# Halving the masked softmax of layer three and reordering the engine queues of a four-layer graph network

## What is computed

```python
x = layernorm(x + L0(x, adj)); x = layernorm(x + L1(x, adj))
x = layernorm(x + L2(x, adj)); x = layernorm(x + L3(x, adj))
# L0, L1: graph attention with one head (softmax over 256 neighbours, masked by adj)
# L2 ("layer three", index 2 in the names): 4 heads of 32 features
def L2(x, adj):
    q, k, v = (x @ Wq + bq), (x @ Wk + bk), (x @ Wv + bv)      # split in 4 heads
    scores = einsum('bnhd,bmhd->bhnm', q, k) / sqrt(32)
    attn = softmax(where(adj | eye, scores, min))              # 4 x 256 x 256 per graph
    return relu(einsum('bhnm,bmhd->bnhd', attn, v) @ Wo + bo)
# L3: gated relational convolution; adj here holds 0 and 1 only
```

## Time and profile before

| | |
|---|---|
| median of 3 runs | 487.91 us (486.52 to 494.0) |
| the profiled execution's own time | 486.33 us |
| its span, first to last instruction | 484.5 us |
| mean granted TensorE clock | 0.995 of full speed |
| DMA | 38.79 MB, mean 80 GB/s |

### The profile page before, as it was taken

One profiled execution on the slowest core, in us unless ns is written; L12 is line 12 of the kernel. 1 busy time (PEld: TensorE's weight loads), 2 busy tenths in 40 slices (PEclk: granted clock), 3 DMA queues, 4 the chain that ended last, 5 costly groups with the idle time before them and its releaser, 6 DMA issues. The chain is left out here.

```text
span 484.5 us, 13810 instructions
## 1 busy us (share of the span) xinstructions
PE 456.0 (94%) x3782; PEld 385.5 (80%) x3782; DVE 420.0 (87%) x1637; ACT 411.8 (85%) x1233; POOL 308.3 (64%) x671
## 2 busy tenths in 40 slices
PE   6868999999999999999999999999999999999863
PEld 5757778888888888898888888888888888887642
DVE  5688998999999999999999999999999999877553
ACT  3659999999999999999999999999999999988720
POOL 1255445566786666677876666677766677765633
PEclk9999999999999999999999999999999999999997
DMA  7532332343423334433323334343322321111122
GB/s 219 124 74 70 73 71 78 89 89 85 95 62 77 83 87 99 101 99 92 82 62 88 79 98 98 99 99 84 81 66 72 99 45 35 33 33 33 37 54 57
DMA packets 60734, 38.79 MB, mean 80 GB/s; under 512 B 11249, under 2 KB 56689, under 8 KB 60658
## 3 DMA queue, kind: packets, MB, share of 16 engines
q1 hardware_dynamic: 60658, 37.89, 32.4%
HBM read 25.24 MB, written 8.45 MB: 70 GB/s over the span
## 5 line engine op out<-in xcount | busy, mean ns | idle before, releaser
L1240 POOL TENSOR_SCALAR x<-y,minus_mean,rstd 128x128 f32<-128x128 f32 x244 | 130.2, 542 | 12.4 <-issue 10.6
L819 ACT ACTIVATE p<-p,nmax 128x256 f32<-128x256 f32 x256 | 127.6, 516 | 0.3 <-DVE nmax L1024 0.3
L1215 POOL TENSOR_SCALAR ve<-stats 128x2 f32<-128x2 f32 x128 | 29.1, 227 | 146.9 <-DVE stats L928 139.4
L1222 POOL TENSOR_TENSOR rstd<-ve,minus_half 128x2 f32<-128x2 f32 x128 | 100.1, 782 | 0.0
L1024 DVE CUSTOM_DVE_ANT_0 p<-ps,neg 128x256 f32<-128x256 f32 x256 | 90.5, 419 | 6.3 <-PE ps L592 6.3
L828 ACT COPY p2T<-ps 128x512 f32<-128x512 f32 x128 | 72.7, 598 | 0.9 <-PE ps L603 0.4
L603 PE MATMUL ps<-ident,p 128*128 128x128 f32 x512 | 71.9, 273 | 1.5 <-DVE nmax L1024 1.1
L737 ACT COPY xT<-ps 128x256 f32<-128x256 f32 x96 | 36.3, 378 | 34.5 <-PE ps L472 34.3
L603 PEld LDWEIGHTS ps<-ident,p 128*128 128x128 f32 x512 | 59.6, 141 | 6.0 <-DVE nmax L1024 1.9
L928 DVE BATCH_NORM_STATS2 stats<-y 128x6 f32<-128x256 f32 x128 | 53.8, 422 | 1.4
L819 ACT ACTIVATION_READ_ACCUMULATOR p<-p,nmax 128x1 f32 x256 | 52.6, 206 | 0.0
(11 more groups left out here) (130 smaller groups left out, 1130.5 us busy)
## 6 DMA issues: line engine op xcount, KB each, us to landing
adj_in<-in_adj_dram SPq DMA_DIRECT2D x32, 256.0 KB, 5.0
s2row<-s_rows SPq DMA_DIRECT2D x29, 256.0 KB, 4.3
xT<-in_xT_dram SPq DMA_DIRECT2D x32, 128.0 KB, 4.7
x_in<-in_x_dram SPq DMA_DIRECT2D x32, 128.0 KB, 5.6
rs_row<-rs_turned SPq DMA_DIRECT2D x64, 64.0 KB
x_aside<-x SPq DMA_DIRECT2D x32, 128.0 KB, 4.8
out_dram<-x SPq DMA_DIRECT2D x32, 128.0 KB, 4.1
s_rows<-xw SPq DMA_DIRECT2D x29, 2.0 KB, 4.2
```

Of the source, the lines that this page charges most:

```text
L819: last = nc.scalar.activation(p2(n)[:, k, a, :], p2(n)[:, k, a, :], ACT.Exp, bias=nmax2(n)[:, k, a:a + 1], scale=-1.0, accum_out=sum2(n)[: ...
L1222: nc.gpsimd.tensor_tensor(rstd[layer](n), ve[layer](n), minus_half[:, :], ALU.pow)\
L1240: last = nc.gpsimd.tensor_scalar(dst[:, k, 0:D], y_t[layer](n)[:, k, :], minus_mean[layer](n)[:, k:k + 1], rstd[layer](n)[:, k:k + 1], ALU ...
```

## The change

The softmax of layer three is cut otherwise. e2 and exp2, so far one step per row half k with four heads, become four steps each, for half k ("a", "b") and head pair ("0", "1"), with two heads each. pT2 and c_pT2, so far one bank per (k, j) with all four heads, take one bank per (k, pair), with two heads and both column halves j. The score bank of a head is released by the steps of its pair. All five queues of PLAN are new. In the rarely run branch for other adjacency values (`relations`), three semaphores of PE and three of ACT are merged; with the inputs here it isn't executed.

On SP, ld_w moves ahead of all loads but first_w; ld_x moves from two places ahead of y0's to the same period; on PE, prep_a comes first, and agg2 stands directly ahead of sc2 of a graph two later. The diff, without the merged semaphores:

```diff
 PLAN = {
-    "sync": [("ld_xT", 5638), ("ld_adj", 6788), ("s2_out", 7405), ("ld_w", 7493), ("s2_in", 8576), ("ld_x", 9221),
-        ("rs_in", 15122), ("aside", 17850), ("store", 20864)],
-    "tensor": [("proj0", 7378), ("s2_rows", 9215), ("prep_a", 9999), ("pT0", 10683), ("agg0", 11226),
-        ("prep_c", 11329), ("prep_b", 11731), ("prep_d", 11822), ("xT1", 11910), ("tT", 12071), ("z1", 12295),
-        ("xw1", 12318), ("pT1", 12938), ("agg1", 13107), ("xT2", 13423), ("qk2", 13601), ("sc2", 13775),
-        ("v2", 14020), ("pT2b0", 14284), ("pT2a1", 14475), ("pT2a0", 14594), ("rs_rows", 14623), ("pT2b1", 15216),
-        ("agg2", 15353), ("wo2", 15683), ("xT3", 17066), ("hg3", 17176), ("agg3", 17378), ("flag", 26327)],
+    "sync": [("ld_w", -9396), ("ld_xT", 6694), ("s2_out", 8145), ("ld_adj", 8179), ("s2_in", 8522), ("ld_x", 10460),
+        ("rs_in", 15434), ("aside", 18797), ("store", 21738)],
+    "tensor": [("prep_a", -10527), ("proj0", 7060), ("s2_rows", 8274), ("prep_c", 8678), ("pT0", 10259),
+        ("prep_d", 10293), ("agg0", 10413), ("prep_b", 11041), ("xT1", 11194), ("tT", 11372), ("z1", 11629),
+        ("xw1", 11927), ("pT1", 12337), ("agg1", 12496), ("xT2", 13812), ("qk2", 14018), ("v2", 14023),
+        ("sc2", 14171), ("pT2b0", 14970), ("rs_rows", 15176), ("pT2a0", 15571), ("pT2b1", 15582), ("pT2a1", 15668),
+        ("agg2", 16139), ("wo2", 16373), ("xT3", 18229), ("hg3", 18970), ("agg3", 19360), ("flag", 21925)],
...
+    "scalar": [("c_prep_a", 1348), ("c_proj0", 7062), ("c_s2", 8369), ("c_prep_c", 8633), ("exp0", 10043),
+        ("c_pT0", 10354), ("c_prep_b", 10542), ("c_prep_d", 11167), ("c_xT1", 11265), ("c_tT", 11473),
+        ("relu1", 11760), ("c_xw1", 11933), ("exp1", 12173), ("c_pT1", 12411), ("c_elu1", 13020), ("c_xT2", 13775),
+        ("c_qk2", 14015), ("c_v2", 14041), ("exp2b0", 14441), ("exp2a1", 14504), ("exp2a0", 14576),
+        ("exp2b1", 14803), ("c_pT2b0", 15013), ("c_rs", 15241), ("c_pT2a0", 15708), ("c_pT2b1", 15755),
+        ("c_pT2a1", 15793), ("c_xT3", 18272), ("gate3", 18809)],
+    "vector": [("masks", 9166), ("e0", 9370), ("m0", 9441), ("neg1", 10215), ("s0", 10471), ("r0", 10627),
+        ("y0", 10682), ("b0", 10853), ("lk1", 11883), ("e1", 12012), ("r1", 12664), ("h1", 12796), ("eq1", 12961),
+        ("y1a", 13044), ("y1b", 13182), ("b1", 13232), ("flag_a", 13805), ("e2b0", 14286), ("e2a1", 14336),
+        ("e2a0", 14400), ("e2b1", 14553), ("r2", 14986), ("onT2", 16203), ("y2a", 16654), ("y2b", 16953),
+        ("b2", 17089), ("end_norm2", 17924), ("vals3", 19001), ("y3", 19382), ("flag_b", 19592), ("b3", 19625),
+        ("end_norm3", 21336)],
+    "gpsimd": [("var0", 10686), ("rsq0", 10841), ("norm0", 11057), ("var1", 13299), ("rsq1", 13345),
+        ("norm1", 13370), ("neg2", 13743), ("var2", 17116), ("rsq2", 17445), ("norm2", 17979), ("var3", 19689),
+        ("rsq3", 20089), ("norm3", 20594)],
 }
...
-    "sc2": [("a", "e2a_ready", "e2b_ready")] * HEADS,
+    "sc2": [("a", f"e2a{a // 2}_ready", f"e2b{a // 2}_ready") for a in range(HEADS)],
...
-            def pT2(k, j, n):
-                step = f"pT2{'ab'[k]}{j}"
+            def pT2(k, pair, n):
+                step = f"pT2{'ab'[k]}{pair}"
                 o = bank(step, n)
                 bank_free(pe, step, n)
-                pe.wait_ge(sem(f"p_ready2{'ab'[k]}"), n + 1)
-                for a in range(HEADS):
-                    last = pe.transpose(o[:, a * P:(a + 1) * P], p2(n)[:, k, a, j * P:(j + 1) * P], ident[:, :])
+                pe.wait_ge(sem(f"p_ready2{'ab'[k]}{pair}"), n + 1)
+                for a in range(2):
+                    for j in range(T):
+                        last = pe.transpose(o[:, (a * T + j) * P:(a * T + j + 1) * P],
+                                            p2(n)[:, k, 2 * pair + a, j * P:(j + 1) * P], ident[:, :])
                 last.then_inc(sem("pT_ps2" + step[3:]), 1)
...
-            def exp2(k, n):
-                half = "ab"[k]
+            def exp2(k, pair, n):
+                half = f"{'ab'[k]}{pair}"
                 act.wait_ge(sem(f"e2{half}_ready"), n + 1)
                 free(act, "small", n, "rsum2_ready")
-                for a in range(HEADS):
+                for a in (2 * pair, 2 * pair + 1):
...
-                nc.scalar.copy(p2T(n)[:, :, j, k * P:(k + 1) * P],
-                               bank("pT2" + half, n).rearrange("p (h i) -> p h i", h=HEADS))\
+                nc.scalar.copy(p2T(n)[:, 2 * pair:2 * pair + 2, :, k * P:(k + 1) * P],
+                               bank("pT2" + half, n).rearrange("p (h j i) -> p h j i", h=2, j=T))\
...
-            def e2(k, n):
+            def e2(k, pair, n):
                 dve.wait_ge(sem("neg2_ready"), n + 1)
-                half = "ab"[k]
-                free(dve, "p2", n, f"pT_ps2{half}0")
-                free(dve, "p2", n, f"pT_ps2{half}1")
+                half = f"{'ab'[k]}{pair}"
+                free(dve, "p2", n, f"pT_ps2{half}")
                 free(dve, "small", n, f"p_ready2{half}")
-                for a in range(HEADS):
+                for a in (2 * pair, 2 * pair + 1):
...
             def r2(n):
-                dve.wait_ge(sem("p_ready2a"), n + 1)
-                dve.wait_ge(sem("p_ready2b"), n + 1)
+                for half in ("a0", "a1", "b0", "b1"):
+                    dve.wait_ge(sem(f"p_ready2{half}"), n + 1)
```

More of the change, by code:

```diff
@@ L26 @@
 PLAN = {
-    "sync": [("ld_xT", 5638), ("ld_adj", 6788), ("s2_out", 7405), ("ld_w", 7493), ("s2_in", 8576), ("ld_x", 9221),
-        ("rs_in", 15122), ("aside", 17850), ("store", 20864)],
[6 rows of a table removed]
-        ("c_prep_c", 11718), ("c_prep_d", 12016), ("c_xT1", 12016), ("c_tT", 12107), ("c_prep_b", 12171),
[12 rows of a table removed]
+    "sync": [("ld_w", -9396), ("ld_xT", 6694), ("s2_out", 8145), ("ld_adj", 8179), ("s2_in", 8522), ("ld_x", 10460),
+        ("rs_in", 15434), ("aside", 18797), ("store", 21738)],
[6 rows of a table added]
+        ("c_pT0", 10354), ("c_prep_b", 10542), ("c_prep_d", 11167), ("c_xT1", 11265), ("c_tT", 11473),
[13 rows of a table added]
 }
@@ L663, in relations @@
                         last = pe.transpose(ps[:, 1, k * P:(k + 1) * P], rel_x[:, k, :], ident[:, :])
-                    last.then_inc(sem("rel_T_ps"), 1)
-                    pe.wait_ge(sem("rel_T_sb"), g + 1)
+                    last.then_inc(sem("rel_pe"), 1)
+                    pe.wait_ge(sem("rel_act"), 3 * g + 1)
                     for way in range(3):
@@ L669, in relations @@
                                              rel_xT[:, k * P:(k + 1) * P], rel_w[:, way, :], start=True, stop=True)
-                    last.then_inc(sem("rel_hg_ps"), 1)
+                    last.then_inc(sem("rel_pe"), 1)
                     pe.wait_ge(sem("rel_loop_vals"), g + 1)
@@ L675, in relations @@
                                              rel_vals[0][:, j, :], start=(j == 0), stop=(j == T - 1))
-                    last.then_inc(sem("rel_loop_ps"), 1)
+                    last.then_inc(sem("rel_pe"), 1)
                     with pe.Fori(0, NREL) as r:
@@ L822, in exp2, with c_pT2 @@
                 last.then_inc(sem(f"p_ready2{half}"), 1)
-            def c_pT2(k, j, n):
-                half = f"{'ab'[k]}{j}"
+            def c_pT2(k, pair, n):
+                half = f"{'ab'[k]}{pair}"
                 act.wait_ge(sem("pT_ps2" + half), n + 1)
                 free(act, "p2T", n, "agg_ps2", HEADS)
-                nc.scalar.copy(p2T(n)[:, :, j, k * P:(k + 1) * P],
-                               bank("pT2" + half, n).rearrange("p (h i) -> p h i", h=HEADS))\
+                nc.scalar.copy(p2T(n)[:, 2 * pair:2 * pair + 2, :, k * P:(k + 1) * P],
+                               bank("pT2" + half, n).rearrange("p (h j i) -> p h j i", h=2, j=T))\
                     .then_inc(sem("pT_sb2" + half), 1)
@@ L843, in relations @@
                 with act.Fori(0, B) as g:
-                    act.wait_ge(sem("rel_T_ps"), g + 1)
+                    act.wait_ge(sem("rel_pe"), 3 * g + 1)
                     nc.scalar.copy(rel_adjT_f.rearrange("p t n -> p (t n)"), ps[:, 0, :])
-                    nc.scalar.copy(rel_xT, ps[:, 1, 0:N]).then_inc(sem("rel_T_sb"), 1)
-                    act.wait_ge(sem("rel_hg_ps"), g + 1)
+                    nc.scalar.copy(rel_xT, ps[:, 1, 0:N]).then_inc(sem("rel_act"), 1)
+                    act.wait_ge(sem("rel_pe"), 3 * g + 2)
                     nc.scalar.copy(rel_hg[:, 0:3].rearrange("p w t d -> p w (t d)"), ps[:, 2:5, :])\
-                        .then_inc(sem("rel_hg_sb"), 1)
+                        .then_inc(sem("rel_act"), 1)
                     act.wait_ge(sem("rel_loop_sum"), g + 1)
                     nc.scalar.activation(rel_hg[:, 2, :, D:2 * D], rel_hg[:, 2, :, D:2 * D], ACT.Tanh, scale=0.5)\
-                        .then_inc(sem("rel_loop_gate"), 1)
+                        .then_inc(sem("rel_act"), 1)
                     with act.Fori(0, NREL) as r:
@@ L866, in _ @@
```

(16 more changed lines are left out.)

## The result

The changed kernel takes 511.99 us (median of 4 runs, 511.47 to 512.9) against 487.89 us for the kernel before (486.52 to 494.0): a ratio of 1.046, 95% interval 1.039 to 1.053. It is slower by 24 us, outside the range of the prediction. The profiled execution took 511.47 us, with a span of 509.7.

The account below looks back on a forecast made before the run. The prediction took PE (TensorE) to bound the middle at 13.73 us a graph; -3.0 + 1.4 + 1.5 + 0.5 - 3.2 = -2.8 us from 487.91 gave 485.1, predicted as 485, range 475 to 497.

Parts of the forecast that it names:

- Do the waits of the new order fit into 13.64?: Middle: engine waits fit PE's 13.64 us period, except one x load chain, charged 0.05 for each of 27 periods.
- +1.4 us for the x load: Middle: landings above the median cost half their excess, 0.05 us for each of 27 periods, +1.4 us.
- the right chain: Middle: rs_rows, c_rs, x load, y0, GpSimd's normalisations, next period's xT1: 13.8 us; with 13.5, 13.65 a period.
- rival 1: Middle: the x load sets the pace; landing 6.4 gives 494.7 us, 7.1 gives 504; chance 20%.
- just in time: Middle, DVE queue behind y0: vals3, whose bank agg2 needs, comes out just in time; no cost charged.
- PE's new order: Middle: agg2 and sc2 become neighbours, saving one boundary's 0.10 us a period, 30 times: -3.0 us (0 to -5.7).
- The halved steps: Layer three's softmax on ACT and DVE: about two added waits per graph on each, priced at nothing in the middle.
- The start: Before graph 0: weights and prep_a come first; +1.5 us (0 to +3.5), first aggregation near 14.6.
- Ramp and drain: Both ends: layer three a stage later, ramp +0.5 us (-2 to +4); more left at qk2.31, drain -3.2 (-5 to 0).
- The last stretch: Drain, from qk2.31 to the end: grows by 1.4 us, from 34.0 to 35.4.

Follow-up runs that it names:

- norm2_early: The changed kernel with norm2 placed earlier in GpSimd's order (17600, was 17979), the x load staying late: 503.69 us, ratio 1.024.
- x_late_loops_cut: The changed kernel with norm2 at 17600 and eq1 moved behind vals3 on DVE, the x load staying late: 498.48 us, ratio 1.021.
- x_early: The changed kernel with the x load a graph earlier, in the same slot behind rs_in: 498.13 us, ratio 1.010.
- loads_ahead: The changed kernel with both the x and xT loads ahead of rs_in in SP's order: 480.35 us, ratio 0.981.

## Why the prediction was wrong

The step that failed is "Do the waits of the new order fit into 13.64?", its term of +1.4 us for the x load, which measured some 24. It was the right chain and the right rule, (chain + 13.5) / 2 against PE's own period, with the wrong size, and it was taken for the only chain. One number of the changed kernel, the x load's place, is worth 511.99 - 487.76 = 24.2 us, as much as the whole loss, and this is shown by the run, not argued; with xT's place as well it is 511.99 - 480.35 = 31.6. How that divides over the following three is in part argued.

**The chain was too short.** It is 15.3, not 13.8. GpSimd's part is most of it. The norm pair takes 2.99 against 2.18 and rsq0 0.89 against 0.80. The 545 ns of the earlier trace rows are a mean of two kinds: in the kernel before such an instruction took 442 ns at the least, 462 at the median and 898 at the most. In the changed kernel the four of the chain take 1.03, 0.72, 0.64 and 0.68 while DVE runs L989, L1011, L932, L914, L1017, L1042 and L920, and the pairs outside it take 0.45 each (the row at 262.35) while DVE runs L1027 and L953. So the time goes with what DVE does beside it; which property of those instructions matters, no run tells.

The landing was 6.08 against 5.6. The place behind rs_in doesn't explain that, since the old x load stood there too:

```profile
254.32 1.15 SPq L359 DMA_DIRECT2D rs_row<-rs_turned  x2
255.51 2.56 SPq L348 DMA_DIRECT2D x_in<-in_x_dram  x1
```

What is new is s2_in (256 KB), now issued right behind x_in; whether it is the cause of the 0.4 us was not tested. What made the load late is that it now stands there with the x of the same period: the old one was issued 32.6 us ahead of its y0, the new one 6.1 (medians of graphs 13 to 28).

So rival 1 was right in kind (20%), by DVE's wait and PE's. Its 494.7 was too low. Its 504 rests on a chain of 15.3, which is the measured one, but by luck: it had 7.1 for the landing and the short GpSimd.

**There were more loops than one.** Behind y0 stood vals3, and "just in time" was my word for it. norm2_early showed it as a loop of 13.94 us, and x_late_loops_cut confirmed it: 0.25 us a period came back when nothing but eq1 was moved behind vals3. In the changed kernel itself this loop shows little, 2.8 us of PE in 6 waits; it becomes the limit once the long one is shortened.

**Another load lost its lead unseen.** By the places xT went from 1.74 periods ahead of proj0 (5638, 7378) to 0.37 (6694, 7060), and in the traces from 24.0 us between issue and proj0 to 5.3. I never priced that. It cost the changed kernel little (1.7 us between 100 and 400, 3.7 in all), since its slow periods gave xT time (a median lead of 5.3 us, against 4.3 in x_early); with x mended it cost x_early 14.6.

**PE's new order** was mis-sized the other way. I took -3.0 (0 to -5.7), the value for a middle boundary that costs like the others. Adjacency gave 0.20 a period, 30 x 0.20 = -6, just past the upper end. With the load in time a period fell by 0.27 in all, to 13.47. For the other 0.07 I have only an argument: the two transposes behind sc2 took 0.28, where half of four (0.43) is 0.22, and now rs_rows stands there with 0.11.

**The halved steps** at nothing: right in the old order's 18 periods, to the hundredth.

**The start**: +1.5 predicted, 1.8 by the trace. The first aggregation was 1.9 later than I said, since prep_a waited 4.57 us for the weights, but half of the 3.5 us was caught up by proj0.13.

**Ramp and drain**, +0.5 and -3.2: in loads_ahead, whose span is 5.6 below before, 30 periods at 0.27 give -8.1 and the start +1.8, so +0.7 is left where I had -2.7. Both parts' bounds cover it. The last stretch was right: 35.4 predicted, 35.6 measured (34.8 in loads_ahead). qk2.31 was expected near 446 and came at 474.11; in loads_ahead it is 444.13. With the loads in time, then, the rest of my sum held within a few us (480 where it said 483.7); with them late it was off by 27.

## What to carry to other kernels

When an order is changed, list for each load how long before its reader it is issued, before and after, and what stands ahead of it in its queue: a load behind something that the bound engine gives late in its period makes a loop through that engine. Follow every signal of the reader, not one: here y0's lateness reached PE through xT1, through vals3's bank and, in the old order, through agg0's bank. Size a loop with the durations of its own instructions, by what runs beside them, and not with a mean over several kinds, take the upper ends, and remember that beyond the point where it decides each us comes back in every period.

## What was unexpected of the hardware

An x load of 128 KB takes SP 2.36 us to issue where it stands right behind rs_in's two transfers and lands after 6.0; ahead of rs_in (loads_ahead, behind adj_in and xT) it is issued in 0.43 and lands after a median of 2.7 between 100 and 400 us. The long issue doesn't vanish, it moves: there xT, right behind adj_in, has 2.21 and lands after 4.3.

```profile
253.31 0.37 SPq L341 DMA_DIRECT2D adj_in<-in_adj_dram  x1
253.73 2.21 SPq L345 DMA_DIRECT2D xT<-in_xT_dram  x1
255.98 0.43 SPq L349 DMA_DIRECT2D x_in<-in_x_dram  x1
257.77 1.17 SPq L360 DMA_DIRECT2D rs_row<-rs_turned  x2
```

And a boundary between column-strip and row-strip products, though its weight loads pause for 0.41 us, adds no time to the two, while a full-size step ahead of strips or behind them takes 0.10 longer.
